# Softmax normalisation moved from the attention output to the probabilities, in three attention phases of a four-layer kernel

## The reference

```python
# layer 0, self and cross (16 heads of 32, 128 keys)
scores = jnp.einsum('bhqd,bhkd->bhqk', q, k) / jnp.sqrt(jnp.float32(HD))
scores = scores * mask - 10000.0 * (1.0 - mask)
probs = jax.nn.softmax(scores, axis=-1)
ctx = jnp.einsum('bhqk,bhkd->bhqd', probs, v)        # then merge_heads(ctx) @ w_o + b_o, + residual
# layer 3, latent (16 heads of 32, 256 keys: 128 of the context, 128 latents)
attn = jnp.einsum('bkhd,bnhd->bhkn', q, kmat) / DH
attn = jnp.where(full_mask[:, None, None, :], attn, -jnp.inf)
attn = jax.nn.softmax(attn.astype(jnp.float32), axis=-1)
attn_out = jnp.einsum('bhkn,bnhd->bkhd', attn, v).reshape(b, k_len, H) @ out_w + out_b + residual
```

## Time and profile before

| what | value |
|---|---|
| median of 3 runs | 3333.68 us (3331.2 to 3334.68) |
| the profiled execution | 3329.89 us, its span 3328.1 us |
| PE busy in the span | 3064.4 us (92%) |
| DVE, ACT, POOL busy | 2076.9 (62%), 1246.6 (37%), 908.1 us (27%) |
| 30 to 351 us, self | 321 us; PE 307.70, DVE 184.25, POOL 115.34 |
| 382 to 705 us, cross | 323 us; PE 306.32, DVE 183.90, POOL 115.23 |
| 2403 to 2907 us, latent | 504 us; PE 484.24, DVE 267.90, POOL 35.28 |

### The profile page before, as it was taken

The page is one execution under the profiler, slowest core; times in us unless marked ns, Lnnn a source line. Parts: engine busy times, 40 slices in busy tenths (PEclk is TensorE's granted clock), DMA queues, the critical chain, the costliest instruction groups (busy, mean ns, idle before and its releaser), DMA issues. The chain is left out here.

```text
span 3328.1 us, 58838 instructions
## 1 busy us (share of the span) xinstructions
PE 3064.4 (92%) x21440; PEld 2230.1 (67%) x21440; DVE 2076.9 (62%) x3074; ACT 1246.6 (37%) x4419; POOL 908.1 (27%) x645
## 2 busy tenths in 40 slices
PE   8999899979999889886899999997799999899999
PEld 5666566658999755555676767674455555489998
DVE  4555455564544477875899999998254464564543
ACT  2444344432322366662343443442243343322322
POOL 2333233340000012223655555566000000030000
PEclk9999899989999999997999999998899999999999
DMA  4110141110000241112111111110130111010010
GB/s 174 42 41 31 54 155 54 49 38 22 17 25 19 80 156 43 50 34 68 46 40 39 51 51 38 39 49 30 64 141 27 33 31 36 28 43 27 30 38 13
DMA packets 104317, 170.31 MB, mean 51 GB/s; under 512 B 16512, under 2 KB 54016, under 8 KB 100736
## 3 DMA queue, kind: packets, MB, share of 16 engines
q1 hardware_dynamic: 99296, 124.58, 11.7%
q10 hardware_dynamic: 4896, 44.04, 3.3%
HBM read 135.03 MB, written 33.55 MB: 51 GB/s over the span
## 5 line engine op out<-in xcount | busy, mean ns | idle before, releaser
L2668 POOL TENSOR_TENSOR rec_S<-rec_S,rec_r_t 128x1024 f32<-128x1024 f32 x128 | 306.1, 2392 | 311.6 <-DVE rec_S L2993 310.7
L2993 DVE TENSOR_TENSOR_SCAN rec_S<-rec_decay,rec_S 128x1024 f32<-128x1024 f32 x128 | 301.3, 2354 | 8.3 <-DVE rec_S L2978 4.2
L1510 ACT ACTIVATE group_scores<-group_scores,group_negmax 128x128 f32<-128x128 f32 x512 | 198.4, 400 | 29.2 <-DVE group_negmax L1605 19.3
L608 ACT ACTIVATE latent_scores<-latent_scores,region_a 128x256 f32<-128x256 f32 x256 | 126.8, 501 | 71.6 <-DVE region_a L795 71.6
L608 ACT ACTIVATE self_scores<-self_scores,self_negmax 128x128 f32<-128x128 f32 x256 | 99.2, 396 | 76.8 <-DVE self_negmax L795 76.8
L608 ACT ACTIVATE cross_scores<-cross_scores,cross_negmax 128x128 f32<-128x128 f32 x256 | 99.2, 396 | 76.4 <-DVE cross_negmax L795 76.4
L2094 ACT ACTIVATE mlp_h_t<-mlp_h_t,vectors 128x128 f32<-128x128 f32 x256 | 81.9, 392 | 120.0 <-DVE mlp_h_t L2189 92.9
L2094 ACT ACTIVATE pmlp_h_t<-pmlp_h_t,vectors 128x128 f32<-128x128 f32 x256 | 81.9, 392 | 119.9 <-DVE pmlp_h_t L2189 94.8
L3298 PE MATMUL rec_rec_out<-rec_S,head_sum 128*32 128x256 f32 x1024 | 84.0, 401 | 46.1 <-POOL rec_S L2668 44.9
L2978 DVE TENSOR_TENSOR rec_S<-rec_vb,rec_k 128x1016 f32<-128x1016 f32 x96 | 115.4, 1202 | 0.0
L979 PE MATMUL latent_pjA<-latent_src_t,F_query_key 128*128 128x512 f32 x240 | 114.4, 600 | 0.0
(11 more groups left out here) (480 smaller groups left out, 7842.6 us busy)
## 6 DMA issues: line engine op xcount, KB each, us to landing
rec_vb<-v_by_head SPq DMA_DIRECT2D x32, 512.0 KB, 4.2
region_a<-in_C_w ACTq DMA_DIRECT2D x2, 4096.0 KB, 19.0
region_a<-in_G_w ACTq DMA_DIRECT2D x2, 4096.0 KB, 19.3
self_xres<-in_x SPq DMA_DIRECT2D x16, 256.0 KB, 2.7
rows_A<-self_xres SPq DMA_DIRECT2D x16, 256.0 KB, 2.0
cross_ctx_t<-in_ctx_t SPq DMA_DIRECT2D x16, 256.0 KB, 3.4
cross_xres<-rows_A SPq DMA_DIRECT2D x16, 256.0 KB, 2.6
rows_B<-cross_xres SPq DMA_DIRECT2D x16, 256.0 KB, 2.0
```

The source lines that it names most:

```text
L608: nc.scalar.activation(S[:, u, at, :], S[:, u, at, :], ACT.Exp, bias=negmax[:, u, at.start // KB:at.start // KB + 1], accum_out=rowsum[:, ...
L1510: nc.scalar.activation(S[:, u, at, :], S[:, u, at, :], ACT.Exp, bias=negmax[:, u, at:at + 1], accum_out=rowsum[:, u // UPS, sum_column(u, ...
L2668: nc.gpsimd.tensor_tensor(S[u % 4][:, :, :], S[u % 4][:, :, :], bcast(r_t[:, s.k, UNITS[u][0], :], [128, JH, T], 1), ALU.mult)\
L2993: nc.vector.tensor_tensor_scan(St[:, :, :].rearrange(flat), decay[m][:, :, :].rearrange(flat), St[:, :, :].rearrange(flat), 0.0, ALU.mult, ...
```

## The change

POOL now multiplies the exponentials in S by the inverse sums, in place, before they are transposed (`scale_probs`): four multiplications of 128x512 per unit in self and cross, two of 128x1024 in latent. Each T(u, r) waits for its multiplication instead of for the exponentials. DVE inverts the sums in smaller pieces and earlier (`invert`: 8 sums, four times per iteration in all three phases). `spread_sums` (8 transposes of PE per iteration), POOL's L545 and DVE's two copies to `ri` go, and the multiplication at the output becomes a copy (`gather`). In self and cross the first half of out(0) moves ahead of T(1,2), and POOL's queue is reordered: the multiplications of unit 0 stand between the bias halves of unit 1.

```diff
@@ body_uses (banks)
-                if u == UPS and r == 0:
+                if u == UPS and r == 0 and grouped:
                     body_uses.append(("PQ"[turn % 2], ("ri", 0), 0))
@@
+        inverses, scalings = (2, 4) if normed else (1, 2)
+        probs_scaled = sem("probs_scaled")
@@ gpsimd
+            def scale_probs(it, u, r):
+                pool.wait_ge(rinv_done, (it * U + u) * inverses + r * inverses // scalings + 1)
+                of = HU * (u % UPS) + 4 * r
+                heads = S[:, u, :, :].rearrange("p (i r b) t -> p i r b t", r=scalings, b=KB)[:, :, r, :, :]
+                inverse = rinv[:, u // UPS, of:of + 4].unsqueeze(2).unsqueeze(3).to_broadcast([128, 4, KB, T])
+                nc.gpsimd.tensor_tensor(heads, heads, inverse, ALU.mult).then_inc(probs_scaled, 1)
...
+            def normed_body(it):
+                add_bias(it, 0, 0)
+                add_bias(it, 0, 1)
+                add_bias(it, 1, 0)
+                scale_probs(it, 0, 0)
+                scale_probs(it, 0, 1)
+                add_bias(it, 1, 1)
+                scale_probs(it, 0, 2)
+                scale_probs(it, 0, 3)
...
+                residual_bias(it, 0)
+                scale_probs(it, 1, 0)
+                scale_probs(it, 1, 1)
+                if has_later(it, 2):
+                    norm_scale(it + 2)
+                scale_probs(it, 1, 2)
+                scale_probs(it, 1, 3)
+                residual_bias(it, 1)
+
+            def latent_body(it):
+                for u in range(U):
+                    if u >= UPS:
+                        residual_bias(it, u - UPS)
+                    for r in range(scalings):
+                        scale_probs(it, u, r)
@@ scalar, exponentials
+                if not grouped:
+                    wait_count(act, rinv_done, ((it - 1) * U + u) * inverses + part * inverses // 2 + 1)
@@ vector
+            def invert(it, u, part=0):
+                of = HU // inverses
+                dve.wait_ge(exp_done, (it * U + u) * HU + (part + 1) * of)
+                wait_count(dve, probs_scaled, ((it - 1) * U + u) * scalings + (part + 1) * scalings // inverses)
+                heads = slice(HU * (u % UPS) + part * of, HU * (u % UPS) + (part + 1) * of)
+                nc.vector.reciprocal(rinv[:, u // UPS, heads], rowsum[:, u // UPS, heads]).then_inc(rinv_done, 1)
+
+            def gather(it, k):
+                dve.wait_ge(pj.full_sem(("pv", k)), pj.uses_with(it, ("pv", k)))
+                nc.vector.tensor_copy(o_t[:, k, :, :].rearrange("p c t -> p (c t)"), pj.bank(("pv", k))[:, :])\
+                    .then_inc(pj.free_sem(("pv", k)), 1)
@@ vector, normed_body
+                invert(it, 0, 0)
                 values(it, 1)
...
                 row_max(it, 1, [0])
+                invert(it, 0, 1)
...
-                invert_sums(it, 0)
+                invert(it, 1, 0)
...
                 copy_probs(it, 1, [0])
-                normalise(it, 0)
-                copy_probs(it, 1, [1, 2, 3])
+                gather(it, 0)
+                copy_probs(it, 1, [1])
+                invert(it, 1, 1)
+                copy_probs(it, 1, [2, 3])
...
-                invert_sums(it, 1)
-                normalise(it, 1)
+                gather(it, 1)
@@ vector, latent_body
                     row_max(it, u)
+                    if u >= UPS:
+                        invert(it, u - UPS)
...
-                copy_probs(it, 1)
-                invert_sums(it, 0)
-                copy_probs(it, 2, [0])
-                normalise(it, 0)
-                copy_probs(it, 2, [1, 2, 3])
+                copy_probs(it, 1, [0, 1, 2])
+                invert(it, 2)
+                copy_probs(it, 1, [3])
+                gather(it, 0)
+                invert(it, 3)
+                copy_probs(it, 2)
@@ tensor
-                pe.wait_ge(exp_done, it * U * HU + u * HU + (4 * (r // 2 + 1) if latent else 4 * (r + 1)))
+                    pe.wait_ge(probs_scaled, (it * U + u) * scalings + r * scalings // 4 + 1)
@@ tensor, normed_body
-                spread_sums(it, 0)
...
                 weigh_values(it, 1, 0)
+                outputs(it, 0, 0)
                 transpose_probs(it, 1, 2)
-                outputs(it, 0, 0)
                 outputs(it, 0, 1)
...
-                spread_sums(it, 1)
```

More of the change, by code:

```diff
@@ L371, in attention_phase @@
         o = sb("o", [128, SL, D]) if grouped else xres
-        ri = sb("ri", [128, D])
-        rinv_by_feature = sb("rinv_by_feature", [128, D])
+        ri = sb("ri", [128, D]) if grouped else None
+        rinv_by_feature = sb("rinv_by_feature", [128, D]) if grouped else None
         o_t = sb("o_t", [128, SL, C, T])
@@ L401, in attention_phase @@
             body_uses += [("A", item, 0 if item[0] == "out" else 1) for item in project[u]]
-        body_uses.append(("PQ"[turn % 2], ("ri", 1), 0))
+        if grouped:
+            body_uses.append(("PQ"[turn % 2], ("ri", 1), 0))
         pj = Banks("pj", sem, {b: ps(f"pj{b}", [128, BANK]) for b in "ABPQ"},
@@ L547, in spread_inverse, with group_body @@
                     .then_inc(rinv_spread, 1)
-            def body(it):
-                if normed:
-                    add_bias(it, 0, 0)
-                    add_bias(it, 0, 1)
+            def normed_body(it):
[7 more added lines that the diff above has]
+                scale_probs(it, 0, 3)
                 if kind == "self" and is_first(it):
                     const["rows_load"].wait(pool)
-                if grouped and not is_first(it):
+                residual_bias(it, 0)
[12 more added lines that the diff above has]
+                        scale_probs(it, u, r)
+            def group_body(it):
+                if not is_first(it):
                     norm_scale(it - 1)
                 residual_bias(it, 0)
-                if normed:
-                    add_bias(it, 1, 0)
-                    add_bias(it, 1, 1)
                 residual_bias(it, 1)
                 spread_inverse(it, 0)
-                if normed and has_later(it, 2):
-                    norm_scale(it + 2)
                 spread_inverse(it, 1)
@@ L570, in _ @@
                 norm_scale(1)
-            run_ahead(pool, body)
+            run_ahead(pool, normed_body if normed else group_body if grouped else latent_body)
             if grouped:
@@ L602, in exponentials @@
             def exponentials(it, u, part):
-                if part == 0 and u % UPS == 0:
+                if not grouped:
+                    wait_count(act, rinv_done, ((it - 1) * U + u) * inverses + part * inverses // 2 + 1)
+                elif part == 0 and u % UPS == 0:
                     wait_count(act, rinv_done, it * 2 + u // UPS - 1)
@@ L1038, in transpose_probs @@
                 begin(it, item)
-                pe.wait_ge(exp_done, it * U * HU + u * HU + (4 * (r // 2 + 1) if latent else 4 * (r + 1)))
+                if grouped:
+                    pe.wait_ge(exp_done, it * U * HU + u * HU + 4 * (r + 1))
+                else:
+                    pe.wait_ge(probs_scaled, (it * U + u) * scalings + r * scalings // 4 + 1)
                 for i, slot in enumerate(slots(r)):
```

## The result

The changed kernel takes 3327.98 us (median of 20 runs, 3321.86 to 3329.78), the kernel before 3332.89 (20 runs, 3329.26 to 3337.64). The medians lie 4.9 us apart. The ratio of the two is 0.9982, with a 95% interval of 0.9975 to 0.9989: 0.18%, or 6 us, faster. That is within 0.2% and inside the range of 3326 to 3347, but on the other side of the forecast of +1.8 us, and the interval leaves "no change" out. The profiled executions took 3329.89 us before and 3328.83 after (spans 3328.1 and 3326.7). Where an execution was plainly disturbed (one of 4568 us and one of 7385 us among those of the last four experiments), it is left out of medians and ratios.

The account below looks back on a forecast made before the run. The prediction took PE to bound the kernel. Its terms, latent -8.2, loops of self and cross +3.1, first iterations +3.9 and eighth iterations +3.0, summed to +1.8 us: predicted 3335 us, range 3326 to 3347.

Parts of the forecast that it names:

- Latent, -8.2: Latent phase: removed transposes return 0.43 + 0.70 = 1.13 us in each of seven iterations, 0.3 in the eighth.
- Self's and cross's loop, +3.1: Self and cross loops: later transposes, mainly T(0,0) and T(1,0), cost +0.26 us per iteration, in 12 iterations.
- I take 1.2, between them: POOL's new 128x512 multiplication: assumed 1.2 us, between L545's 1.04 and L538's 1.28.
- the removed 0.43 and the moved 0.43: Self and cross loops: 0.43 us from unit 0's removed spread transposes cancels 0.43 for T(1,2) moved behind out(0)'s first half.
- First iterations, +1.9 each: First iterations of self and cross: queries start at 47.31 instead of 45.40, +1.9 us each, +3.9 for two.
- Eighth iterations, +1.5 each: Eighth iterations of self and cross: 1.5 us lost once more to the lower PE clock, +3.0 together.
- my upper bound of 4.8: Eighth iterations of self and cross: four multiplications wholly exposed, +4.8 us; the lower bound was -2.0.
- The smaller way to the faster side: POOL at 1.04 or less and eighth iterations at their lower bound: -8.1 us, 3326; result below -0.2% had chance 0.2.
- POOL over 1.3 us: Slower rival: POOL's multiplication takes over 1.3 us, so T(0,2) waits too; at 1.5 about +22, 3356; chance 0.19.
- latent at half: Slower rival: DVE's extra inversions hold latent's scores, the 0.7 do not return; +4.9, sum +6.7, 3340; chance 0.08.
- both spread groups returning: Faster rival: both spread groups come back everywhere, 17 us less, 3318; result below -0.2% had chance 0.2.
- The rule against the change: POOL multiplying beside DVE's L706: the port rule would start POOL up to 1.0 us late, taking only slack ahead of T(1,2).

Follow-up runs that it names:

- t12_first: The changed kernel with T(1,2) put back ahead of out(0) in self and cross: 3322.59 us, ratio 0.9965 against the kernel before.
- both_orders: On top of `t12_first`, the first half of queries(0) ahead of T(0,0) in self's and cross's first iteration: 3321.75 us, ratio 0.9962 against the kernel before.
- before_again: The kernel before, run again with nothing edited for a second trace: 3334.03 us, ratio 0.9999.
- after_res_first: The changed kernel with POOL's residual bias 1 back right behind residual bias 0 in self and cross: 3336.28 us, ratio 1.0006 against the kernel before.

## Why the prediction was wrong, step by step

**Latent, -8.2: right, a little too large.** Alone it gave -7. In the second to fifth iterations it is 0.94 to 0.97 each: 0.53 of the second group's 0.70 and the 0.43 of the first. PE has 0.17 us of "issue" before the scores there, which the spread's transposes had covered. In the first, sixth and seventh, it is the 1.19 to 1.20 that I had worked out as 1.13, so I put the difference down to the loop's back edge (the jump to its start); no run tests that. The eighth gave nothing back, where I had 0.3: 474.56 us from its scores to the end, against 474.08.

**Self's and cross's loop, +3.1: too large.** The step "I take 1.2, between them" failed by its size: the multiplication takes 1.04. My own working gives +0.06 per iteration for that; the traces show 245.11 us before and 244.91 after for self's second to eighth start, -0.03 per iteration, and cross's third to seventh within 0.2 us of before in sum. It is 3 us too much in a sum of +1.8, so this term alone set the forecast's sign. That the removed 0.43 and the moved 0.43 cancel is borne out by `t12_first`, where the moved one comes back as 0.41.

**First iterations, +1.9 each: too small.** They grew by 3.3 (by 1.6 in cross against the 40.85 that it has in most traces of before). PE in self's, after:

```profile
46.11 0.85 PE L1094 MATMUL self_pjP<-ident,self_scores 128*128 128x128 f32 x4 [4.03 <-POOL self_scores L551]
46.75 3.40 PE L1010 MATMUL self_pjA<-self_src_t,region_a 128*128 128x256 f32 x8
```

The place of the queries was worked out well: 47.31, less the 0.5 by which self starts earlier in this execution, is 46.8, and they start at 46.75. What I left out is that an idle stretch of 4.03 us costs the clock. It is 0.57 from 46 to 50:

```profile
46.00:50.00 4.00, 3.89 (x13) 3.21 (x14) 1.93 (x3) 1.37 (x8) 4.00 (x3) 0.57 0.00 0
```

The queries' eight matmuls take 3.40 us and not 1.97; that 1.43 is what is missing. `both_orders`, in which PE starts the queries without waiting for POOL, is 2.4 us shorter and has its clock at 1.00. The 40.85 us of cross in the other traces of before are the clock too: with the same waits of 1.48 and 0.69 us, the queries' matmuls take 2.86 in `before_again` and 1.96 in the first trace.

**Eighth iterations, +1.5 each: the number right, by luck.** They grew by 1.4 (self) and 1.7 (cross). I had read a clock loss of 1.5 us in the old kernel and taken it as lost once more, and did not ask what brought it. The residual bias ahead of the spread did: with it last these iterations take 38.95 and 40.21 us, and against that the change costs 5.9 and 4.7, in self more than my upper bound of 4.8. One loss took the place of another: in the changed kernel POOL's multiplications are what PE waits for, and `after_res_first` shows that the place of the residual bias gives nothing there. PE in self's eighth iteration, after:

```profile
333.22 0.63 PE L1094 MATMUL self_pjP<-ident,self_scores 128*128 128x128 f32 x4 [1.20 <-POOL self_scores L551]
...
337.54 1.09 PE L1094 MATMUL self_pjP<-ident,self_scores 128*128 128x128 f32 x4 [2.33 <-POOL self_scores L551]
...
342.36 1.09 PE L1094 MATMUL self_pjP<-ident,self_scores 128*128 128x128 f32 x4 [0.66 <-POOL self_scores L551]
...
345.45 3.78 PE L1057 MATMUL self_pjA<-region_a,self_o_t 128*128 128x512 f32 x4
```

The three waits are 4.2 us, and four matmuls of out(0) take 3.78 where the loop's take 1.98. The granted clock, by stretches of 4 us, is the lower of the two levels (0.50, 1.2 GHz) from 338 to 350:

```profile
334.00:338.00 4.00, 1.45 (x15) 1.07 (x16) 3.59 (x5) 3.00 (x16) 4.00 (x4) 0.81 0.44 133
338.00:342.00 4.00, 3.50 (x31) 1.55 (x30) 1.49 (x3) 4.00 (x22) 2.45 (x3) 0.50 0.01 2
...
346.00:350.00 4.00, 4.00 (x9) 1.87 (x8) 0.00 (x0) 0.00 (x0) 2.81 (x3) 0.50 0.00 0
```

Behind it cross opens 0.9 us later than before, with its first features' 16 matmuls at 6.42 us (5.66 before); the forecast had nothing there.

**The step that failed.** "Cross has the same body as self and I count it as the same." It has the same body, but not the same neighbours: in its second iteration the next phase's weights fill the DMA engines, and POOL waits 14.21 us for one load. The residual bias has a row in the loop of self, "[5.23 <-DMA self_xres<-in_x]", which I quoted for its duration and did not read to the end: it says that POOL stands there until a transfer lands, with spread 0 behind it. The change lifts it out of the way. The forecast counted the reordering of POOL's queue by which multiplication comes late, and never asked what comes early. The term +0.26 for cross's second iteration was -3.6 in the trace shown and -5.2 and -5.4 against the other two of the old order. That the result's sign hangs on this is shown by `after_res_first`: with the move undone the ratio is 1.0006, +2 us. This happens to be the +1.8 of the forecast, but by luck: its terms were off by up to 5 us, on both sides.

**The sum again.** By the stretches of the two traces, after minus before: self's first +3.3, its loop -0.2, its eighth +1.4, opening of cross +0.9, cross's first +3.3 and second -3.6, the later ones +0.1, its eighth +1.7, latent -7.4 and +0.5 behind it: 0.0. The untouched stretches make the 1.4 in the spans; they differ by up to 8 us between executions. Against the `before_again` trace cross's first and second iterations are +1.6 and -5.2, and the sum of all these stretches becomes -3.1, inside the spread but short of the -4.9 of the medians. Where the rest lies is open. The forecast's own range was added up wrongly, too: its bounds give -8.1 and about +10.4, where it says -7 to +8.

**The rivals.** POOL over 1.3 us fell by L551's 1.04, latent at half by its -7, both spread groups returning by the scores that still wait for ACT. The smaller way to the faster side, POOL at 1.04, held in the loop alone; its eighth iterations at the lower bound did not. So the kernel got faster by a mechanism that none of them named.

**The rule against the change.** The Trainium skill's "SBUF — State Buffer", on the shared port pair, says that a DVE operation in a two-port mode and a GpSimd operation exclude each other: the later one waits for the whole instruction of the other. POOL and DVE in the loop, after:

```profile
184.83 2.44 POOL L551 TENSOR_TENSOR self_scores<-self_scores,self_rinv 128x512 f32<-128x512 f32 x2 [2.32 <-DVE self_rinv L850]
```

```profile
184.67 1.71 DVE L738 TENSOR_SCALAR self_xn<-self_x,self_stats,self_rstd 128x512 f32<-128x512 f32 x2
```

Alone, two multiplications take 2.04 us and the two normalisations took 1.00. Side by side POOL loses 0.40 and DVE 0.71, POOL less than the up to 1.0 us that I allowed for. The single instructions in these rows (ns, minimum/median/maximum, then the first and last start):

```profile
L738 DVE TENSOR_SCALAR self_xn<-self_x,self_stats,self_rstd x2: 530/898/1265, 184.7 to 185.1; 128x512 f32<-128x512 f32 x2
L551 POOL TENSOR_TENSOR self_scores<-self_scores,self_rinv x2: 1216/1241/1266, 184.8 to 186.1; 128x512 f32<-128x512 f32 x2
```

The first normalisation, which started first, takes its usual 530 ns; the first multiplication, begun beside it, takes 1266 instead of 1040; the second normalisation starts 0.3 us into that multiplication, takes 1265 instead of 540, and ends 0.3 us behind the multiplication's end; the second multiplication takes 1216. So whichever starts second is held up, one instruction at a time, and both engines pay in turn. The trace agrees with the Trainium skill in this; whether L738 runs in such a mode no row says. Nothing on PE waited for either in the loop, as the slack behind out(0)'s first half said.

## What to carry to other kernels

Ask of each instruction on an in-order engine what it waits for before asking what it costs, and of each repeated phase which foreign transfers pass through it: one bias addition in the wrong place of POOL's queue cost 13 us in the kernel before and would have cost 8 in the changed one, more than the change gained. When an edit is a bundle, price each reordering in it as its own edit, those that look like tidying too, and don't expect the prices to add up: 13 became 8 once another wait stood in its place. Where PE is left waiting, ask what its next matmuls lose at half the clock. That was 1.4 us behind a wait of 4.03, 3.3 us behind one of 1.44, and between nothing and 1.8 us behind waits of 3.4 and 3.2 in two executions of one kernel, so it is a range and not a number.

## What had not been expected of the hardware

- A POOL multiplication of 128x512 with one full operand and one repeated along the row takes 1.04 us, as one with both repeated does; an addition with two full ones takes 1.26 to 1.29. At 128x1024 the multiplication takes 1.89 against the 2.36 of the addition L532, whose second operand repeats a block of 128 different values. No run tells the operation from the operand.
- When POOL and DVE meet with two instructions each, both engines are slowed (2.04 to 2.44 and 1.00 to 1.71), since each holds up the other's next instruction.
- PE shows 0.17 us of issue before the first scores of a loop iteration in latent, which came to light once the transposes ahead of them were gone (1.20 returned where there is no back edge, 0.95 where there is).
- With one wait of PE at 0.36 us instead of 1.44, the granted clock in self's eighth iteration stayed at 1.00 where it had been 0.50, worth three times the difference in the wait. Self's eighth iteration is 43.3 to 43.5 us in all three traces of the old order and 38.95 and 39.21 in the two of the new one. In cross's, with the same 0.36 us, the second projection still took 5.37 us.
